# The second plane of a unit in two VectorE instructions: one bank, then two banks

## The chip, the cores and the metric

One core of one Trainium2 chip runs the whole program. The time is the device time of that core in microseconds (us); the kernel before was run three times and the median counts. Tensors lie in SBUF (128 partitions) and in PSUM, 128 partitions with 8 banks of 512 fp32 each. Engines: TensorE (PE; its weight loads PEld), VectorE (DVE), ScalarE (ACT), GpSimd (POOL), SyncE (SP, which issues the DMAs). They run side by side and meet only at semaphores.

## The reference

A decoder of two layers on 32 batches of 56 tokens with a context of 1500 rows, width 128: self attention, cross attention, experts, a state-space block, the second cross attention and experts again. The change is in the second cross attention:

```python
xn = _layernorm(x, ln_gamma, ln_beta)
q = (xn @ w_q).reshape(B, SQ, NUM_HEADS, DIM_HEAD)      # 32, 56, 16 heads, 64
kv = context @ w_kv                                     # 32, 1500, ...
k, v = jnp.split(kv, 2, axis=-1)
...
scores = jnp.einsum('bqhd,bkhd->bhqk', q * SCALE, k)
attn = jax.nn.softmax(scores, axis=-1)
out = jnp.einsum('bhqk,bkhd->bqhd', attn, v).reshape(B, SQ, INNER)
out = out @ w_out + b_out
return out * jnp.tanh(gate[0])
```

## The kernel before

`cross_attention_phase` multiplies the queries by the key weights beforehand, so that scores come straight from the context, and applies value and output weights behind the attention. A *unit* is 128 rows of scores (8 tokens by 16 heads) by 1500 context columns. A batch has 7 units, a pair of batches 14 (NU), and there are 16 pairs, 224 units in all. The first and the last pair are written out, the 14 between are a loop; inside a pair the position s runs from 0 to 13.

Scores of unit s stand in three PSUM banks, 500 columns in each: banks 0 to 2 for even s, 3 to 5 for odd s (`bank = 3 * (s % 2)`). A unit goes through these steps:

- TensorE, `scores` (L2098 to L2100): for each bank three matmuls, high by high, high by low and low by high parts. Ahead of the group of bank j it waits on `h2_ready` until unit s-2, which used the same bank, is done with it.
- VectorE, `maximum`: a maximum over two banks (L2226) as soon as they are there, then one over the third bank and the first result (L2230).
- ScalarE, `exponentials` (L2344): the exponentials of all three banks in place, with their sum.
- VectorE, `inverse` (L2235, L2237): the sum's reciprocal.
- ScalarE, `high_part` (L2360): the normalised probabilities in fp16 into plane 0 of `h`, in two instructions: banks 0 and 1, then bank 2. Each adds to `h1_ready`.
- VectorE, `low_part` (L2245): probability times reciprocal minus plane 0 gives the rest, plane 1 of `h`, in three scalar_tensor_tensor instructions of one bank each. Each adds one to `h2_ready`, and with that frees its bank for unit s+2.
- SyncE transposes `h` by DMA into `prT` (L1971) once all of `h2_ready` is there; for two units of a pair TensorE transposes (`turn`, L2148, in three rounds of eight) and VectorE copies (`keep_turned`, L2251).
- TensorE, `values` (L2123 to L2125): probabilities by context, seven units behind.

The order on each engine is written by hand in its `step`. TensorE in position s: scores of s, a third or a quarter of the value matmuls of a group, then at some positions something more: projection of the next pair's queries (L2083, positions 2 to 5), output matmuls of the previous pair (L2158, positions 7 to 9), its transpose and logits (positions 12 and 13), a turn (positions 0, 1, 6, 10, 11, 13). VectorE in position s: `inverse` of s-1, copies of a turn (positions 0, 1, 2, 7, 11, 12), at position 10 the residual, `maximum` of s, `low_part` of s-1, at position 11 the normalisation.

Of the kernel before, what the change touches and what calls it, by code (L numbers as in the profile page):

```python
# [21 lines left out]
ALU = mybir.AluOpType  # L22
# [19 lines left out]
def this(i, n=1, per=1):  # L42

    return i * per + (per + n)
# [136 lines left out]
def open_sems(engine, per, *sems):  # L181

    for s in sems:
        engine.sem_inc(s, per)
# [1651 lines left out]
def cross_attention_phase(k):  # L1836

    nc = k.nc
    W = C // 3
    UQ = 128 // H1  # L1840
    UPS = S // UQ
    NU = 2 * UPS
# [9 lines left out]
    H_SLOT = [0, 1, 2, 0, 3, 1, 2, 0, 1, 2, 0, 3, 1, 2]  # L1852
# [6 lines left out]
    SCALE = DH1 ** -0.5  # L1859
    P_ONE, N_ONE, TINY = 16384.0, 8192.0, 1.0e-25  # L1860
    PIECES = [(j * W, (j + 1) * W) for j in range(3)]
    with ExitStack() as ctx:
        t = Tail(k, ctx, "xa", router=k.router1, per=1)
        sem = lambda name: k.sem(ctx, "xa_" + name)
# [6 lines left out]
        h = sb("h", [128, 4, 2, CP], fp16)  # L1871
        prT = sb("prT", [128, 2 * GA + UPS - GA, 2 * KT, 128], fp16)
        ident16 = sb("ident16", [128, 128], fp16)
        negmax, rs, rinv = sb("negmax", [128, 2, 1]), sb("rs", [128, 2, 1]), sb("rinv", [128, 2, 1])
# [4 lines left out]
        psum = ctx.enter_context(nc.psum_tensor("xa_psum", [128, 8, 512], fp32))  # L1879
# [8 lines left out]
        h1_ready, h2_ready = sem("h1_ready"), sem("h2_ready")  # L1888
# [53 lines left out]
        @block.sync  # L1942
        def _(sp):
            def load_T(i, h_):

                sp.wait_ge(c_lo_ready, this(i, h_, 2))
                sp.sem_inc(issuing, 1)
                sp.dma_start(ctxT[:, :].unsqueeze(1),
                             k.dram["ctxT"][bass.ds(2 * i + h_, 1), :, :].rearrange("b d c -> d b c"))\
                    .then_inc(ctxT_loaded, 16)  # L1950

            def load_P(i, h_):

                sp.wait_ge(n_lo_ready, this(i, h_, 2))
                sp.sem_inc(issuing, 1)
                sp.dma_start(ctxP[:, :].unsqueeze(1),
                             k.dram["ctxP"][bass.ds(2 * i + h_, 1), :, :, :].rearrange("b q t d -> q b (t d)"))\
                    .then_inc(ctxP_loaded, 16)

            def transpose(i, s):  # L1960

                sp.wait_ge(h2_ready, this(i, 3 * s + 3, 3 * NU))
                sp.sem_inc(issuing, 1)
                b, u = s // UPS, s % UPS

                if u < GA:
                    sp.wait_ge(pv_ready, last(i, 2 * b + 1, NG))
                else:
                    sp.wait_ge(pv_ready, this(i, 2 * b, NG))
                sp.sem_inc(issuing, 1)  # L1970
                sp.dma_start_transpose(prT[:, P_SLOT[s], :, :], h[:, H_SLOT[s], :, :].rearrange("p a c -> p (a c)"))\  # L1971
                    .then_inc(transposed[s], 16)

            def step(i, s, end=False):
                if s not in TURNED:
                    transpose(i, s)
                if s == 1 and not end:
                    load_T(i + 1, 0)
                if s == 4:
                    load_P(i, 1)  # L1980
                if s == 8 and not end:
                    load_T(i + 1, 1)
                if s == 11 and not end:
                    load_P(i + 1, 0)

            load_T(0, 0)
            load_P(0, 0)
            load_T(0, 1)
            with sp.Fori(0, PAIRS - 1) as i:
                for s in range(NU):  # L1990
                    step(i, s)
            for s in range(NU):
                step(PAIRS - 1, s, end=True)
# [78 lines left out]
        def _(pe):  # L2072
# [14 lines left out]
            def scores(i, s):  # L2087
                b, p0, bank = s // UPS, (s % UPS) * UQ, 3 * (s % 2)
                if s % UPS == 0:
                    pe.wait_ge(q_lo_ready, this(i, b + 1, 2))  # L2090
                    pe.wait_ge(c_lo_ready, this(i, b + 1, 2))
                qh = q_hi[:, b, p0:p0 + UQ, :].rearrange("p a b -> p (a b)")
                ql = q_lo[:, b, p0:p0 + UQ, :].rearrange("p a b -> p (a b)")
                for j, (a, z) in enumerate(PIECES):

                    pe.wait_ge(h2_ready, this(i, 3 * (s - 2) + j + 1, 3 * NU))
                    out = psum[:, bank + j, 0:W]
                    nc.tensor.matmul(out, qh, c_hi[:, b, a:z], start=True, stop=False)  # L2098
                    nc.tensor.matmul(out, qh, c_lo[:, b, a:z], start=False, stop=False)  # L2099
                    done = nc.tensor.matmul(out, ql, c_hi[:, b, a:z], start=False, stop=True)  # L2100
                    if j:
                        done.then_inc(scores_ready, 1)
# [26 lines left out]
            def turn(i, u, r, first=False, end=False):  # L2129

                if r:
                    pe.wait_ge(turn_kept[u], this(i, r, NR))
                else:
                    pe.wait_ge(h2_ready, this(i, 3 * u + 3, 3 * NU))
                if u == TURNED[0] and r == 0:
                    pe.wait_ge(turn_kept[TURNED[1]], last(i, NR, NR))
                    if not end:
                        pe.wait_ge(q_kept, q_count(i + 1, NB - 1))
                if u == TURNED[0] and r == 1 and not first:
                    pe.wait_ge(t.r_ready, this(i - 1))  # L2140
                if u == TURNED[1] and r == 0:
                    pe.wait_ge(turn_kept[TURNED[0]], this(i, NR, NR))
                    if not first:
                        pe.wait_ge(t.logits_kept, this(i - 1))
                for j in range(KT // NR):
                    for x in range(2):
                        kt = r * (KT // NR) + j
                        done = nc.tensor.transpose(turn_bank[:, j, x, :], h[:, H_SLOT[u], x, kt * 128:(kt + 1) * 128],  # L2148
                                                   ident16[:, :])
                done.then_inc(turn_ready[u], 1)  # L2150
# [64 lines left out]
        @block.vector  # L2215
        def _(dve):
            open_sems(dve, NU, two_ready, max_ready, total_ready, rinv_ready)
            open_sems(dve, 3 * NU, h2_ready)
            open_sems(dve, NR, *turn_kept.values())
            t.open_vector(dve)  # L2220

# [17 lines left out]
            def low_part(i, s):  # L2239
                bank = 3 * (s % 2)  # L2240
                dve.wait_ge(rinv_ready, this(i, s + 1, NU))
                for j, (a, z) in enumerate(PIECES):
                    if j != 1:
                        dve.wait_ge(h1_ready, this(i, 2 * s + (1 if j == 0 else 2), 2 * NU))
                    nc.vector.scalar_tensor_tensor(h[:, H_SLOT[s], 1, a:z], psum[:, bank + j, 0:W], rinv[:, s % 2, :],  # L2245
                                                   h[:, H_SLOT[s], 0, a:z], ALU.mult, ALU.subtract).then_inc(h2_ready, 1)

            def keep_turned(i, u, r):

# [336 lines left out]
```

## Time and profile before

| | us |
|---|---|
| median of three runs | 1936.44 |
| lowest, highest | 1933.33, 1942.58 |
| the profiled execution | 1935.19 |
| its span, first to last instruction | 1933.5 |
| TensorE busy (share of the span) | 1715.1 (89%) |
| VectorE busy | 1557.1 (81%) |
| ScalarE busy | 1184.6 (61%) |
| GpSimd busy | 797.9 (41%) |
| the 672 instructions of L2245 | 452.6 |
| the 224 of L2226 and the 224 of L2230 | 269.6 and 154.9 |

Busy time is a sum over the program; which engine an end waits for has to be read stage by stage. The chain of work that ended last covers only the very end of the program here (its shares read 0%), so it says nothing on this stage. A matmul's duration on the page overlaps the next one's; the distance between starts is what a matmul costs in a row of many. The second cross attention takes more than half of the span.

### The profile page before, as it was taken

To read this page: it belongs to the slowest core of one execution; us is meant where nothing else is said; L and a number is where in the kernel's file an instruction comes from. 1 tells how busy PE (TensorE), PEld (TensorE's weight loads), DVE (VectorE), ACT (ScalarE), POOL (GpSimd) and SP (SyncE) were. 2 spreads that over 40 slices of the span, in tenths; PEclk is the share of its full clock that TensorE was granted. 3 is DMA by queue.
4 is the path that set the end of the run, shared out by engine and by line. 5 is a ranking of instruction groups with operands and counts; after the bars stand their busy time and mean duration, and the time that the engine had idled before them with its cause. 6 is when DMAs were issued, how large, how long until landed. Compare 5 with 4: busy or idle time off the path is not lost. (4 is left out here: it accounts for less than half of the span.)

```text
span 1933.5 us, 33921 instructions
## 1 busy us (share of the span) xinstructions
PE 1715.1 (89%) x10135; PEld 1224.0 (63%) x10135; DVE 1557.1 (81%) x2940; ACT 1184.6 (61%) x1869; POOL 797.9 (41%) x674
## 2 busy tenths in 40 slices
PE   4887996899946599999999999999999999994997
PEld 2554665777722457666666766666676676663886
DVE  4985785677756498998899899889989988985886
ACT  2432332787721477777777777777777777764553
POOL 4640111233332554554636445463544536321333
PEclk9987998799976699999999999999999999997998
DMA  5202884221100398888898888989888898983231
GB/s 184 93 0 100 328 335 183 57 54 45 23 1 0 100 208 188 187 178 196 175 192 180 186 187 178 200 172 193 178 186 188 178 197 175 183 154 116 47 78 29
DMA packets 632491, 281.86 MB, mean 146 GB/s; under 512 B 602076, under 2 KB 606460, under 8 KB 631676
## 3 DMA queue, kind: packets, MB, share of 16 engines
q1 hardware_dynamic: 632428, 281.10, 62.4%
q8 instruction: 30, 0.49, 0.1%
q14 instruction: 33, 0.27, 0.0%
HBM read 129.02 MB, written 1.05 MB: 67 GB/s over the span
## 5 line engine op out<-in xcount | busy, mean ns | idle before, releaser
L2344 ACT ACTIVATE xa_psum<-xa_psum,xa_negmax 128x1500 f32<-128x1500 f32 x224 | 332.7, 1485 | 197.0 <-DVE xa_negmax L2230 197.0
L2245 DVE SCALAR_TENSOR_TENSOR xa_h<-xa_psum,xa_rinv,xa_h 128x500 f16<-128x500 f32 x672 | 452.6, 729 | 0.7 <-ACT xa_h L2360 0.7
L2360 ACT ACTIVATE xa_h<-xa_psum,xa_rinv 128x1000 f16<-128x1000 f32 x448 | 372.1, 882 | 82.5 <-DVE xa_rinv L2237 81.2
L2226 DVE TENSOR_REDUCE xa_psum<-xa_psum 128x1 f32<-128x1000 f32 x224 | 269.6, 1204 | 86.8 <-PE xa_psum L2100 86.7
L2098 PE MATMUL xa_psum<-xa_c_hi,xa_q_hi 128*128 128x500 f32 x672 | 282.1, 420 | 29.2 <-DVE xa_h L2245 19.0
L2123 PE MATMUL xa_psum<-xa_prT,xa_n_hi 128*128 128x512 f16 (+1 forms) x768 | 272.9, 355 | 1.8 <-issue 1.0
L2125 PE MATMUL xa_psum<-xa_prT,xa_n_lo 128*128 128x512 f16 (+1 forms) x768 | 270.7, 352 | 0.0
L2124 PE MATMUL xa_psum<-xa_prT,xa_n_hi 128*128 128x512 f16 (+1 forms) x768 | 270.7, 352 | 0.0
L2100 PE MATMUL xa_psum<-xa_c_hi,xa_q_lo 128*128 128x500 f32 x672 | 261.7, 389 | 0.0
L2099 PE MATMUL xa_psum<-xa_c_lo,xa_q_hi 128*128 128x500 f32 x672 | 261.5, 389 | 0.0
L2230 DVE TENSOR_REDUCE xa_negmax<-xa_psum 128x1 f32<-128x512 f32 x224 | 154.9, 692 | 25.8
L2017 POOL CAST xa_q_hi<-xa_q_full 128x896 fp32r<-128x896 f32 x32 | 29.8, 931 | 346.6 <-PE xa_psum L2100 335.6
L2098 PEld LDWEIGHTS xa_psum<-xa_c_hi,xa_q_hi 128*128 128x128 f32 x672 | 127.0, 189 | 72.2 <-DVE xa_h L2245 32.4
L1432 DVE TENSOR_TENSOR moe_hid_lo<-moe_hid,moe_hid_hi 128x448 fp32r<-128x448 f32 x200 | 125.2, 650 | 39.5 <-ACT moe_hid_hi L1551 34.1
L2100 PEld LDWEIGHTS xa_psum<-xa_c_hi,xa_q_lo 128*128 128x128 f32 x672 | 126.6, 188 | 26.0
L2123 PEld LDWEIGHTS xa_psum<-xa_prT,xa_n_hi 128*128 128x128 f16 x768 | 76.0, 99 | 103.7 <-issue 54.3
L2037 POOL TENSOR_SCALAR xa_ctxP<-xa_ctxP,xa_n_scale 128x1536 f32<-128x1536 f32 x32 | 133.3, 4167 | 17.8 <-DMA xa_ctxP<-in_ctxP 17.8
L2099 PEld LDWEIGHTS xa_psum<-xa_c_lo,xa_q_hi 128*128 128x128 f32 x672 | 127.4, 190 | 11.4
L2125 PEld LDWEIGHTS xa_psum<-xa_prT,xa_n_lo 128*128 128x128 f16 x768 | 75.1, 98 | 70.0
L1288 POOL TENSOR_TENSOR moe_acc<-moe_acc,moe_part 128x448 f32<-128x448 f32 x52 | 63.5, 1220 | 117.0 <-DVE moe_part L1475 62.6
L2030 POOL TENSOR_TENSOR xa_c_lo<-xa_ctxT,xa_c_hi 128x1500 fp32r<-128x1500 f32 x32 | 107.9, 3373 | 2.6
L2124 PEld LDWEIGHTS xa_psum<-xa_prT,xa_n_hi 128*128 128x128 f16 x768 | 75.5, 98 | 49.1
(304 smaller groups left out, 3465.3 us busy)
## 6 DMA issues: line engine op xcount, KB each, us to landing
ctxN<-in_ctxP SPq DMA_DIRECT2D x16, 1536.0 KB, 9.2
xa_ctxP<-in_ctxP SPq DMA_DIRECT2D x32, 768.0 KB, 4.3
ctxT<-in_ctxT SPq DMA_DIRECT2D x16, 1500.0 KB, 6.2
xa_ctxT<-in_ctxT SPq DMA_DIRECT2D x32, 750.0 KB, 4.7
moe_spread<-weight_rows SPq DMA_DIRECT2D x16, 1024.0 KB, 8.6
xa_prT<-xa_h SPq DMA_TRANSPOSE x192, 5.5
up<-in_F_up SPq DMA_DIRECT2D x1, 2048.0 KB, 9.2
down<-in_F_down SPq DMA_DIRECT2D x1, 2048.0 KB, 13.3
```

The costliest lines, as they stand in the source:

```text
L2037: pool.tensor_scalar(ctxP[:, :], ctxP[:, :], n_scale[:, :], None, ALU.mult).then_inc(n_scaled, 1)
L2098: nc.tensor.matmul(out, qh, c_hi[:, b, a:z], start=True, stop=False)
L2099: nc.tensor.matmul(out, qh, c_lo[:, b, a:z], start=False, stop=False)
L2100: done = nc.tensor.matmul(out, ql, c_hi[:, b, a:z], start=False, stop=True)
L2123: nc.tensor.matmul(out, nh, ph, start=(kt == 0), stop=False)
L2124: nc.tensor.matmul(out, nh, pl, start=False, stop=False)
L2125: done = nc.tensor.matmul(out, nl, ph, start=False, stop=(kt == KT - 1))
L2226: nc.vector.tensor_reduce(psum[:, bank + 1, W:W + 1], psum[:, bank:bank + 2, 0:W], AX.XY, ALU.max)\
L2230: nc.vector.tensor_reduce(negmax[:, s % 2, :], flat_psum[:, top:top + 512], AX.X, ALU.max, negate=True)\
L2245: nc.vector.scalar_tensor_tensor(h[:, H_SLOT[s], 1, a:z], psum[:, bank + j, 0:W], rinv[:, s % 2, :], h[:, H_SLOT[s], 0, a:z], ALU.mult, AL ...
L2344: nc.scalar.activation(psum[:, bank:bank + 3, 0:W], psum[:, bank:bank + 3, 0:W], ACT.Exp, bias=negmax[:, s % 2, :], accum_out=rs[:, s % 2, ...
L2360: nc.scalar.activation(h[:, H_SLOT[s], 0, a * W:z * W].rearrange("p (a c) -> p a c", c=W), psum[:, bank + a:bank + z, 0:W], ACT.Identity, ...
```

## The change

`low_part` makes plane 1 in two instructions: bank 0 alone, then banks 1 and 2 in one, with 1000 columns. Each waits for the ScalarE instruction with that count (`h1_ready`), so the wide one waits for plane 0 of bank 2 before it begins. `h2_ready` now rises by two per unit and no longer by three; TensorE's groups of the second and the third bank wait for the same count. All others that wait for a whole unit (the DMA transpose, the turn) count two. Nothing else is moved, and the arithmetic is the same.

```diff
+    LOW_PIECES = ((0, 1), (1, 3))
+    NL = len(LOW_PIECES)
...
-                sp.wait_ge(h2_ready, this(i, 3 * s + 3, 3 * NU))
+                sp.wait_ge(h2_ready, this(i, NL * (s + 1), NL * NU))
...
-                    pe.wait_ge(h2_ready, this(i, 3 * (s - 2) + j + 1, 3 * NU))
+                    pe.wait_ge(h2_ready, this(i, NL * (s - 2) + min(j + 1, NL), NL * NU))
...
-                    pe.wait_ge(h2_ready, this(i, 3 * u + 3, 3 * NU))
+                    pe.wait_ge(h2_ready, this(i, NL * (u + 1), NL * NU))
...
-            open_sems(dve, 3 * NU, h2_ready)
+            open_sems(dve, NL * NU, h2_ready)
...
-                for j, (a, z) in enumerate(PIECES):
-                    if j != 1:
-                        dve.wait_ge(h1_ready, this(i, 2 * s + (1 if j == 0 else 2), 2 * NU))
-                    nc.vector.scalar_tensor_tensor(h[:, H_SLOT[s], 1, a:z], psum[:, bank + j, 0:W], rinv[:, s % 2, :],
-                                                   h[:, H_SLOT[s], 0, a:z], ALU.mult, ALU.subtract).then_inc(h2_ready, 1)
+                for j, (a, z) in enumerate(LOW_PIECES):
+                    dve.wait_ge(h1_ready, this(i, 2 * s + j + 1, 2 * NU))
+                    high, low = (h[:, H_SLOT[s], x, a * W:z * W].rearrange("p (a c) -> p a c", c=W) for x in range(2))
+                    nc.vector.scalar_tensor_tensor(low, psum[:, bank + a:bank + z, 0:W], rinv[:, s % 2, :], high,
+                                                   ALU.mult, ALU.subtract).then_inc(h2_ready, 1)
```

VectorE in the loop, one position, before (`xa_h` is `h`, `xa_psum` the PSUM banks, `xa_rinv` the reciprocal):

```order
L2226 TENSOR_REDUCE xa_psum<-xa_psum 128x1
L2228 REGISTER_ALU
L2229 REGISTER_ALU
L2230 TENSOR_REDUCE xa_negmax<-xa_psum 128x1
L2245 SCALAR_TENSOR_TENSOR xa_h<-xa_psum,xa_rinv,xa_h 128x500 x3
L2235 TENSOR_SCALAR xa_total<-xa_rs 128x1
L2237 RECIPROCAL xa_rinv<-xa_total 128x1
```

The same place in the changed program:

```order
L2228 TENSOR_REDUCE xa_psum<-xa_psum 128x1
L2230 REGISTER_ALU
L2231 REGISTER_ALU
L2232 TENSOR_REDUCE xa_negmax<-xa_psum 128x1
L2247 SCALAR_TENSOR_TENSOR xa_h<-xa_psum,xa_rinv,xa_h 128x500
L2247 SCALAR_TENSOR_TENSOR xa_h<-xa_psum,xa_rinv,xa_h 128x1000
```

Three rows of 500 columns have become one of 500 and one of 1000; what stands around them is the same.

TensorE in the loop, the scores of one unit, before (`REGISTER_ALU` of L2096 works out the count that the next group waits for):

```order
L2096 REGISTER_ALU
L2098 MATMUL xa_psum<-xa_c_hi,xa_q_hi 128x500
L2099 MATMUL xa_psum<-xa_c_lo,xa_q_hi 128x500
L2100 MATMUL xa_psum<-xa_c_hi,xa_q_lo 128x500
L2096 REGISTER_ALU
L2098 MATMUL xa_psum<-xa_c_hi,xa_q_hi 128x500
L2099 MATMUL xa_psum<-xa_c_lo,xa_q_hi 128x500
L2100 MATMUL xa_psum<-xa_c_hi,xa_q_lo 128x500
L2096 REGISTER_ALU
L2098 MATMUL xa_psum<-xa_c_hi,xa_q_hi 128x500
L2099 MATMUL xa_psum<-xa_c_lo,xa_q_hi 128x500
L2100 MATMUL xa_psum<-xa_c_hi,xa_q_lo 128x500
```

And in the changed program:

```order
L2098 REGISTER_ALU
L2100 MATMUL xa_psum<-xa_c_hi,xa_q_hi 128x500
L2101 MATMUL xa_psum<-xa_c_lo,xa_q_hi 128x500
L2102 MATMUL xa_psum<-xa_c_hi,xa_q_lo 128x500
L2098 REGISTER_ALU
L2100 MATMUL xa_psum<-xa_c_hi,xa_q_hi 128x500
L2101 MATMUL xa_psum<-xa_c_lo,xa_q_hi 128x500
L2102 MATMUL xa_psum<-xa_c_hi,xa_q_lo 128x500
L2100 MATMUL xa_psum<-xa_c_hi,xa_q_hi 128x500
L2101 MATMUL xa_psum<-xa_c_lo,xa_q_hi 128x500
L2102 MATMUL xa_psum<-xa_c_hi,xa_q_lo 128x500
```

No matmul has moved; the third group has no count of its own any more, since it waits for the same one as the second.

## Rows read from the trace of the kernel before

**Rows 1.** Windows: bounds, length, busy us (instructions), PEclk, DMA share, GB/s.

```profile
656.00:1733.00 1077.00, 1056.01 (x6015) 728.59 (x6015) 974.46 (x1736) 807.33 (x1108) 539.29 (x279) 1.00 0.88 183
1121.50:1189.30 67.80, 67.10 (x388) 46.41 (x386) 61.12 (x110) 50.66 (x71) 34.39 (x19) 1.00 0.88 185
660.00:670.00 10.00, 6.36 (x34) 5.22 (x34) 9.49 (x17) 8.37 (x13) 9.75 (x4) 1.00 0.60 94
670.00:680.00 10.00, 7.42 (x39) 6.07 (x40) 9.54 (x17) 9.26 (x15) 0.62 (x1) 1.00 1.02 236
```

**Rows 2.** Timeline (start, duration, instruction): pair's first scores, position 5, next pair.

```profile
1121.53 0.48 PE L2098 MATMUL xa_psum<-xa_c_hi,xa_q_hi 128*128 128x500 f32 x1
1144.27 2.02 DVE L2245 SCALAR_TENSOR_TENSOR xa_h<-xa_psum,xa_rinv,xa_h 128x500 f16<-128x500 f32 x3
1145.59 0.48 PE L2098 MATMUL xa_psum<-xa_c_hi,xa_q_hi 128*128 128x500 f32 x1
1147.24 1.21 DVE L2226 TENSOR_REDUCE xa_psum<-xa_psum 128x1 f32<-128x1000 f32 x1 [0.68 <-PE xa_psum L2100]
1149.18 2.02 DVE L2245 SCALAR_TENSOR_TENSOR xa_h<-xa_psum,xa_rinv,xa_h 128x500 f16<-128x500 f32 x3
1150.49 0.48 PE L2098 MATMUL xa_psum<-xa_c_hi,xa_q_hi 128*128 128x500 f32 x1
1189.39 0.49 PE L2098 MATMUL xa_psum<-xa_c_hi,xa_q_hi 128*128 128x500 f32 x1
```

**Rows 3.** Waits of the whole program: waiting <- awaited, us in total, times, longest.

```profile
DVE xa_psum L2226 <- PE xa_psum L2100: 86.7, 115, 22.9
PEld xa_psum L2098 <- DVE xa_h L2245: 32.4, 56, 3.2
PE xa_psum L2098 <- DVE xa_h L2245: 19.0, 24, 2.8
```

**Rows 4.** Timeline of position 13 of the pair before that one.

```profile
1113.71 1.66 ACT L2360 ACTIVATE xa_h<-xa_psum,xa_rinv 128x1000 f16<-128x1000 f32 x2 [0.91 <-DVE xa_rinv L2237]
1116.09 2.02 DVE L2245 SCALAR_TENSOR_TENSOR xa_h<-xa_psum,xa_rinv,xa_h 128x500 f16<-128x500 f32 x3
1116.88 0.50 PE L2098 MATMUL xa_psum<-xa_c_hi,xa_q_hi 128*128 128x500 f32 x1 [0.61 <-DVE xa_h L2245]
1117.62 0.19 ACT L2344 ACTIVATION_READ_ACCUMULATOR xa_psum<-xa_psum,xa_negmax 128x1 f32 x1
1117.67 0.39 PE L2098 MATMUL xa_psum<-xa_c_hi,xa_q_hi 128*128 128x500 f32 x1
1118.03 0.14 DVE L2235 TENSOR_SCALAR xa_total<-xa_rs 128x1 f32<-128x1 f32 x1
1118.35 0.38 PE L2098 MATMUL xa_psum<-xa_c_hi,xa_q_hi 128*128 128x500 f32 x1
1118.55 1.21 DVE L2226 TENSOR_REDUCE xa_psum<-xa_psum 128x1 f32<-128x1000 f32 x1 [0.18 <-PE xa_psum L2100]
```

**Rows 5.** Groups by line and form: count, busy us, mean ns, idle before.

```profile
L2245 DVE SCALAR_TENSOR_TENSOR xa_h<-xa_psum,xa_rinv,xa_h 128x500 f16<-128x500 f32 x672 | 452.6, 729 | 0.7 <-ACT xa_h L2360 0.7
L1475 DVE SCALAR_TENSOR_TENSOR moe_part<-moe_psum,down_bias,moe_spread 128x448 f32<-128x448 f32 x28 | 19.1, 681 | 6.4 <-PE moe_psum L1348 5.7 <-issue 0.3
L2259 DVE SCALAR_TENSOR_TENSOR xa_r<-xa_psum,gate_tanh,xa_xg 128x128 f32<-128x128 f32 x16 | 5.6, 351 | 14.6 <-PE xa_psum L2158 14.5
L2226 DVE TENSOR_REDUCE xa_psum<-xa_psum 128x1 f32<-128x1000 f32 x224 | 269.6, 1204 | 86.8 <-PE xa_psum L2100 86.7
L2230 DVE TENSOR_REDUCE xa_negmax<-xa_psum 128x1 f32<-128x512 f32 x224 | 154.9, 692 | 25.8
```

**Rows 6.** Timeline of the first unit, where VectorE was free.

```profile
658.63 0.19 ACT L2344 ACTIVATION_READ_ACCUMULATOR xa_psum<-xa_psum,xa_negmax 128x1 f32 x1
658.86 0.15 DVE L2235 TENSOR_SCALAR xa_total<-xa_rs 128x1 f32<-128x1 f32 x1 [1.67 <-ACT xa_psum L2344]
```

**Rows 7.** Timeline of the first pair, positions 3 and 4.

```profile
665.24 2.02 DVE L2245 SCALAR_TENSOR_TENSOR xa_h<-xa_psum,xa_rinv,xa_h 128x500 f16<-128x500 f32 x3
666.03 0.50 PE L2098 MATMUL xa_psum<-xa_c_hi,xa_q_hi 128*128 128x500 f32 x1 [1.11 <-DVE xa_h L2245]
667.70 1.21 DVE L2226 TENSOR_REDUCE xa_psum<-xa_psum 128x1 f32<-128x1000 f32 x1 [0.18 <-PE xa_psum L2100]
670.33 0.49 PE L2098 MATMUL xa_psum<-xa_c_hi,xa_q_hi 128*128 128x500 f32 x1 [1.12 <-DVE xa_h L2245]
```

## The prediction

> **What bounds the kernel now.** I read the busy time by stretch first, then the waits, then the timeline of single units. The second cross attention runs from about 652 to 1740 us. In it TensorE was busy 1056 of 1077 us, VectorE 974, ScalarE 807, and TensorE's granted clock was 1.00, its 2.4 GHz level [rows 1]. One pair of batches (14 units, positions 0 to 13) takes 67.86 us, from the start at 1121.53 to the one at 1189.39 [rows 2]; TensorE is busy 67.10 of 67.80 us there, VectorE 61.12 [rows 1]. So TensorE sets the pace in most positions, and VectorE only now and then: TensorE waits for the second plane of a unit (L2245) 80 times, 51.4 us in all, and VectorE waits for scores 115 times, 86.7 us [rows 3].
>
> The timeline shows both kinds of position. Call L the start of the first L2245 of unit s-2, which frees the banks that unit s needs, and "lead" the start of the scores of unit s minus L. At position 13 VectorE is last: L is 1116.09, the scores start at 1116.88 and have waited [rows 4]. So a finished bank (0.73 us long) is seen 0.06 us after its end, at L+0.79. At position 5 TensorE is last: L is 1144.27, the scores start at 1145.59 (lead 1.32), and the next ones 4.90 us later, with no gap [rows 2]. Read in the same way, the leads of the pair are 0.96, 0.78, 0.79, 0.95, 1.31, 1.31, 1.31, 0.92, 1.48, 1.52, 1.52, 0.83, 0.79, 0.78 for positions 0 to 13 (14 pairs of rows, of which [rows 2] has position 5 and [rows 4] position 13 of the pair before). Only those at 0.78 and 0.79 wait for the first bank.
>
> **Part 1, one instruction less.** Three L2245 lie 0.646 us apart: (2.02-0.73)/2, with a single one of 729 ns [rows 4, 5]. An instruction of two banks is not in the trace. Scalar_tensor_tensor takes 351 ns for 128 columns and 681 for 448 [rows 5], 1.03 ns per column; 729 plus 500 columns gives 1.245. The maximum over the same two banks and 1000 columns takes 1204 against 692 for 512 [rows 5], 1.05 per column, so reading over two banks costs nothing extra; that gives 1.254. I take 1.25. Bounds: 1.19 by the slope between 448 and 500 columns (48 ns for 52), and 1.375, two narrow ones (0.646+0.729), if nothing is saved. The wide one then holds VectorE for 1.25-0.729+0.646 = 1.167 us in place of 1.292. Saved: 0.125 us per unit, 224 units, 28.0 us of VectorE.
>
> Does the next instruction profit? It waits for ScalarE's sum. When VectorE was free, it began 0.04 us after that sum's end (658.63+0.19 to 658.86) [rows 6]; at position 13 the sum ends at 1117.81 and it began at 1118.03 [rows 4], so it can come 0.18 us earlier, and the whole 0.125 is usable. The second wait of the new form (ScalarE's third bank, before the wide one rather than before the third) is covered: the second ScalarE instruction had ended at 1113.71+1.66 = 1115.37, before L = 1116.09 [rows 4]. What this is worth alone: the waits of TensorE at the four positions with lead 0.78 to 0.79 come to 1.15 us per pair, start to start (67.80-67.10 is 0.70, to which the tails of four overlapping matmuls are added). Walking the pair with banks freed as before and VectorE 0.125 faster gives 67.2 for 67.7, so 8 us over the phase.
>
> The Trainium skill, page "VectorE: DVE Perf Modes", section "The TRN2 errata — SBUF-src ops pay a fixed extra latency per instruction", says that the fixed cost lies between instructions and that a large tile pays it once. The three rows 0.646 us apart agree as to the fixed part. Followed alone it would have the change gain what VectorE saves.
>
> **Part 2, the release of banks.** Scores of unit s go bank by bank, three matmuls each. TensorE needs the second bank 0.79 us after its start when it waited, 0.77 when it didn't, and the third 0.68 later [rows 4]. Before, the second bank was free at L+0.646+0.729+0.06 = L+1.43, always in time. Now it comes with the third, at L+0.646+1.25+0.06 = L+1.95. A scores start with lead x therefore stalls for 1.95-(x+0.77) where that is positive: 0.40 us at 0.78, 0.35 at 0.83, 0.26 at 0.92, nothing from 1.18 on. To it comes a restart of 0.10: the first matmul after a wait takes 0.50 and its group 0.79, where a group in the flow takes 0.68 [rows 4] (bound below: 0). Queued behind the stalled matmul are the rest of the scores, the value matmuls, projections and turns of that position, and VectorE's maximum, which needs the second bank's scores: it starts 0.88 after the second bank's first matmul (1117.67 to 1118.55) [rows 4]. The maximum then holds up ScalarE's exponentials and everything of the next unit.
>
> **The sum.** I walked the 14 positions: TensorE's own time in each (4.90 with a projection, the others from start to start in the same manner), the scores not before L+0.78, the maximum 0.88 behind, the next L another 1.93 to 1.94 behind the maximum (1147.24 to 1149.18) [rows 2], VectorE's other steps as they are. For the kernel before, this gives 67.70 us per pair against 67.86 measured: 66.55 of own work and 1.15 of waits. For the changed one the leads settle at 1.08, 1.02, 1.05, 1.42, 1.32, 1.32, 1.32, 0.91, 1.83, 1.52, 1.52, 0.85, 1.01, 0.78. The stalls with restarts are 0.20, 0.25, 0.23 at positions 0 to 2, 0.37 at 7, 0.43 at 11, 0.26 at 12 and 0.50 at 13, together 2.24, and 0.08 of the old wait is left: 66.55+2.24+0.08 = 68.87. So a pair loses 1.17 us, and 14 inner pairs 16.4.
>
> In the first pair TensorE has no value matmuls for seven positions and waits in almost all: L 665.24, scores 666.03, maximum 667.70, next scores 670.33, a position every 4.30 us [rows 7]. Now the maximum can start at L+1.95+0.88 = L+2.83, not L+2.46, so each such position costs 0.37. There are ten of them in the first pair and five in the last (no projections): 5.6. Sum: 22.0 us on the profiled execution's span of 1933.5, so 1955.5; the whole execution had 1935.19 and the median of the three runs is 1936.44, 2.9 above the span: 1958.4.
>
> **The rivals.** (a) The wide instruction is shorter than I think. At 1.19 the walk gives +15, without the restart cost +12: 1949. For: the shallow slope up to 500 columns. Against: 1.05 ns per column over two banks [rows 5].
> (b) It ends on the other side: VectorE sets the pace and the late release costs nothing. That needs the second bank by L+1.55, a wide instruction of 0.85 us, or TensorE always more than 1.18 behind L. Then only part 1 is left: -8 us, 1928; with all of TensorE's 1.15 per pair and the gaps of the first pair it could reach -20, 1917. This is what the skill's rule taken alone would give. For it: 80 waits of TensorE for VectorE. Against: seven of 14 leads are under 1.0.
> (c) Gain and loss cancel: at a wide instruction of 1.03 us the walk breaks even, 1936. No row is near that.
> (d) Two banks in one instruction save nothing (1.375): the walk gives +38, 1974. Against: the maximum's rows.
> That the clock falls through the new stalls is not among them: from 660 to 680 us TensorE was busy 64 to 74% and had 1.00 [rows 1].
>
> **How the numbers follow.** A measurement here tells 0.5%, 9.7 us, from no change. Forecast 0.66 (slower), (a) 0.12 (slower, a third of it within 0.5%), (b) 0.10 (0.04 of it faster by over 0.5%, the rest within), (c) 0.07 (within), (d) 0.05 (slower). That makes faster 0.04, same 0.16, slower 0.80. The range goes from 1944, below (a), to 1967, which takes a wide instruction of 1.30.
>
> **What would show it.** The new row of 128x1000 at 1.25 us; VectorE's busy time down by 28; waits of TensorE at the second bank's first matmul, none of which exist now, seven per pair, about 0.1 to 0.5 us each; those at the first bank nearly gone; VectorE's wait for scores not smaller although it has less to do; pairs of 68.9 us. A pair under 67.9 or no waits at the second bank would prove the step on the release wrong.

## The result and the profile after

The changed kernel takes **1966.95 us** (median of four runs, 1965.76 to 1971.38). Four runs of the kernel before, on the same chip, have a median of 1938.31 (1933.33 to 1942.58). The ratio is 1.0153 with a 95% interval of 1.0122 to 1.0183: slower by 28.6 us, where 22.0 were forecast. The profiled execution took 1971.38 us, its span is 1969.5.

First the busy time by stretch, one pair of batches and then the whole stage; the columns are those of [rows 1].

```profile
1100.00:1169.40 69.40, 68.39 (x386) 45.87 (x385) 59.87 (x96) 50.47 (x70) 34.47 (x18) 1.00 0.86 181
656.00:1733.00 1077.00, 1050.27 (x5819) 699.61 (x5820) 924.01 (x1462) 778.51 (x1075) 534.81 (x275) 1.00 0.86 179
```

In one pair VectorE is busy for 59.87 us, where it was 61.12. The second row is the same stretch of time as before and not the same work: the changed kernel gets less far in it, so only part of the step from 974 to 924 us is work saved. TensorE still has its 2.4 GHz (1.00) over the stage as a whole. Then the forms of L2247 (L2245 before), the maximum and the waits, against [rows 5] and [rows 3]. Columns: busy us, mean ns | idle before it, and for the waits us in total, times, longest.

```profile
L2247 DVE SCALAR_TENSOR_TENSOR xa_h<-xa_psum,xa_rinv,xa_h 128x1000 f16<-128x1000 f32 x224 | 279.9, 1250 | 0.0
L2247 DVE SCALAR_TENSOR_TENSOR xa_h<-xa_psum,xa_rinv,xa_h 128x500 f16<-128x500 f32 x224 | 163.2, 729 | 0.7 <-ACT xa_h L2362 0.7
L2228 DVE TENSOR_REDUCE xa_psum<-xa_psum 128x1 f32<-128x1000 f32 x224 | 270.4, 1207 | 136.1 <-PE xa_psum L2102 130.5
```

```profile
ACT xa_psum L2346 <- DVE xa_negmax L2232: 251.7, 224, 11.8
DVE xa_psum L2228 <- PE xa_psum L2102: 130.5, 155, 22.9
PEld xa_psum L2100 <- DVE xa_h L2247: 84.0, 149, 2.8
PE xa_psum L2100 <- DVE xa_h L2247: 16.6, 47, 2.4
```

VectorE's instruction count and time fell, and the waits for the release and for the maximum grew. The two rows of TensorE for plane 1 come to 196 waits and 100.6 us, where they were 80 and 51.4. (Each of the two sums adds the waits of weight loads and of matmuls, which stand side by side: at 1137.91, in the next timeline, one stall counts 0.64 us for the load and 0.23 for the matmul. So they show the direction, not the time lost.) VectorE waits for scores 130.5 us, not 86.7.

The timeline of position 13 (start, duration, instruction; the counterpart of [rows 4]) shows where.

```profile
1135.96 1.90 DVE L2247 SCALAR_TENSOR_TENSOR xa_h<-xa_psum,xa_rinv,xa_h 128x500 f16<-128x500 f32 x2
1136.74 0.49 PE L2100 MATMUL xa_psum<-xa_c_hi,xa_q_hi 128*128 128x500 f32 x1 [0.15 <-DVE xa_h L2247]
1137.48 0.19 ACT L2346 ACTIVATION_READ_ACCUMULATOR xa_psum<-xa_psum,xa_negmax 128x1 f32 x1
1137.77 0.14 DVE L2237 TENSOR_SCALAR xa_total<-xa_rs 128x1 f32<-128x1 f32 x1
1137.91 0.50 PE L2100 MATMUL xa_psum<-xa_c_hi,xa_q_hi 128*128 128x500 f32 x1 [0.23 <-DVE xa_h L2247]
1138.70 0.38 PE L2100 MATMUL xa_psum<-xa_c_hi,xa_q_hi 128*128 128x500 f32 x1
1138.90 1.21 DVE L2228 TENSOR_REDUCE xa_psum<-xa_psum 128x1 f32<-128x1000 f32 x1 [0.78 <-PE xa_psum L2102]
```

L is 1135.96. The first bank's scores start at L+0.78, as before. The second bank's start at L+1.95, 1.17 behind the first bank's and no longer 0.79, and VectorE is idle for 0.78 us before the maximum may begin. Position 3 of the next pair is one whose scores come late enough to find all three banks free:

```profile
1155.55 1.90 DVE L2247 SCALAR_TENSOR_TENSOR xa_h<-xa_psum,xa_rinv,xa_h 128x500 f16<-128x500 f32 x2
1156.86 0.47 PE L2100 MATMUL xa_psum<-xa_c_hi,xa_q_hi 128*128 128x500 f32 x1
1157.62 0.39 PE L2100 MATMUL xa_psum<-xa_c_hi,xa_q_hi 128*128 128x500 f32 x1
1158.29 0.39 PE L2100 MATMUL xa_psum<-xa_c_hi,xa_q_hi 128*128 128x500 f32 x1
1158.49 1.21 DVE L2228 TENSOR_REDUCE xa_psum<-xa_psum 128x1 f32<-128x1000 f32 x1 [0.79 <-PE xa_psum L2102]
```

Put side by side, the two timelines hold what the prediction left out. In both the maximum starts 0.20 us after the third bank's first matmul (1138.70 to 1138.90, 1158.29 to 1158.49). From the second bank's first matmul to the third's it is 0.67 us in position 3 (1157.62 to 1158.29), but 0.79 in position 13 (1137.91 to 1138.70), where that first matmul has waited and takes 0.50. So the maximum comes 0.99 us behind the second bank's first matmul where that has waited, and 0.87 where it hasn't.

A pair now takes 69.44 us, from maximum to maximum (the median of the inner pairs); before it was 67.83. The whole stage is bounded by the first and the last maximum (columns: shortest, median and longest ns, then first and last start). Before:

```profile
L2226 DVE TENSOR_REDUCE xa_psum<-xa_psum x224: 1189/1208/1208, 655.2 to 1726.3; 128x1 f32<-128x1000 f32 x112
```

After:

```profile
L2228 DVE TENSOR_REDUCE xa_psum<-xa_psum x224: 1189/1208/1208, 660.1 to 1762.7; 128x1 f32<-128x1000 f32 x112
```

That is 1071.1 and 1102.6 us: 31.5 longer. Another 4.9 of the 36.0 us between the two spans lie ahead of the first maximum, in code that is the same in both. The last section comes back to them; the profiled execution was the longest of its four.

### The profile page after: what moved, and what is told of

Its sections match the earlier page's. It is cut to its first block and busy times, and to the rows that moved or that the text cites. A ratio compares the mean times of both kernels' runs of the same rounds, so it can differ in the third digit from the quotient of the medians.

```text
span 1969.5 us, 33501 instructions
## 1 busy us (share of the span) xinstructions
PE 1744.6 (89%) x10135; PEld 1218.7 (62%) x10135; DVE 1538.4 (78%) x2716; ACT 1181.2 (60%) x1869; POOL 798.1 (41%) x674
## 5 line engine op out<-in xcount | busy, mean ns | idle before, releaser
L2247 DVE SCALAR_TENSOR_TENSOR xa_h<-xa_psum,xa_rinv,xa_h 128x500 f16<-128x500 f32 x448 | 424.6, 989 | 0.7 <-ACT xa_h L2362 0.7
L2228 DVE TENSOR_REDUCE xa_psum<-xa_psum 128x1 f32<-128x1000 f32 x224 | 270.4, 1207 | 136.1 <-PE xa_psum L2102 130.5
L2100 PE MATMUL xa_psum<-xa_c_hi,xa_q_hi 128*128 128x500 f32 x672 | 294.7, 439 | 35.0 <-DVE xa_h L2247 16.6
## 6 DMA issues: line engine op xcount, KB each, us to landing
down<-in_F_down SPq DMA_DIRECT2D x1, 2048.0 KB, 13.4
```

Source lines behind the costliest of these rows:

```text
L2228: nc.vector.tensor_reduce(psum[:, bank + 1, W:W + 1], psum[:, bank:bank + 2, 0:W], AX.XY, ALU.max)\
L2247: nc.vector.scalar_tensor_tensor(low, psum[:, bank + a:bank + z, 0:W], rinv[:, s % 2, :], high, ALU.mult, ALU.subtract).then_inc(h2_ready, 1)
```

## The experiments

Two theories differ in one point. **Theory 1**, formed from the two timelines above: the late release sets the time, and a score group that has waited runs 0.11 us longer, so that the maximum of that unit is later by as much, and with it everything of the next unit. A unit whose second bank waits then can't take less than 1.95 to the release, 0.99 to the maximum and 1.93 to the next L: 4.87 us. **Theory 1a** is the prediction's: the same without that delay (0.88, so 4.76). **Theory 2**: not the release but the wide instruction as such makes the kernel slower, wherever it stands. For Theory 1 and 1a I walked the 14 positions as in the prediction. Since the 0.99 was read from the changed kernel's own trace, only the kernels below can test it. Each is compared with runs of the kernel before on its own chip.

**Late release without the wide instruction.** The kernel before, with its three narrow instructions; only the second bank's scores wait for the third one.

```diff
-                    pe.wait_ge(h2_ready, this(i, 3 * (s - 2) + j + 1, 3 * NU))
+                    pe.wait_ge(h2_ready, this(i, 3 * (s - 2) + (3 if j else 1), 3 * NU))
```

> The kernel before, with its three one-bank instructions untouched; only TensorE's group of the second bank waits for the third instruction, as its third group does. So VectorE saves nothing and the release is late: L+0.646+0.646+0.729+0.06 = L+2.08. Theory 1 (the late release costs, and the restart of 0.10 delays the second bank's scores too, so that a position with lead 0.78 takes 2.08+0.98+1.93 = 4.99 us from L to L): the walk gives 70.2 us per pair and +47 us. Theory 1a (the restart counts for TensorE alone, as in the prediction): 69.8 per pair, +39. Theory 2 (the instruction over two banks is itself the cost, whatever waits for it): no such instruction here, so 0.

Measured: 1988.09 us against 1937.04, ratio 1.0257 (1.0242 to 1.0273), so 51 us slower, and 70.7 us per pair. Its timeline in a position with a late start of scores:

```profile
1103.93 2.02 DVE L2245 SCALAR_TENSOR_TENSOR xa_h<-xa_psum,xa_rinv,xa_h 128x500 f16<-128x500 f32 x3
1105.24 0.47 PE L2098 MATMUL xa_psum<-xa_c_hi,xa_q_hi 128*128 128x500 f32 x1
1106.01 0.49 PE L2098 MATMUL xa_psum<-xa_c_hi,xa_q_hi 128*128 128x500 f32 x1
1106.99 1.21 DVE L2226 TENSOR_REDUCE xa_psum<-xa_psum 128x1 f32<-128x1000 f32 x1 [0.78 <-PE xa_psum L2100]
```

No wide instruction runs here, and a wait on the release alone costs more than the whole change did. Theory 2, which had 0, falls. The release is at L+2.08 (1103.93 to 1106.01), which is 0.77 after the scores' start, just when TensorE wants the bank. The matmul comes no later than in the flow, and still the maximum is 0.98 behind: its group pays the 0.11 of one that has waited. What waited was the weight load of this group (last section). That makes each of these units 2.08+0.98+1.94 = 5.00 us; measured are 4.99 to 5.02 in ten of the 14 positions. The walk of Theory 1 took such a tie for free at positions 3 to 6; four times 0.11 more makes its 70.2 us per pair 70.6, for 70.7 measured. That is worked out afterwards and explains most of the step from 47 to 51. Theory 1a's 39 is further off.

**The wide instruction first.** Banks 0 and 1 are made together, then bank 2; the total saved on VectorE is the same.

```diff
-    LOW_PIECES = ((0, 1), (1, 3))
+    LOW_PIECES = ((0, 2), (2, 3))
...
-                    pe.wait_ge(h2_ready, this(i, NL * (s - 2) + min(j + 1, NL), NL * NU))
+                    pe.wait_ge(h2_ready, this(i, NL * (s - 2) + max(j, 1), NL * NU))
```

> The changed kernel with the wide instruction first (banks 0 and 1, then bank 2), TensorE's first two groups waiting for the first. VectorE's saving and the number of wide instructions are as in the changed kernel. Theories 1 and 1a: TensorE waits once, ahead of the first bank, until L+1.25+0.06 = L+1.31, and then runs through; the cycle at a waiting position is 1.31+0.79+0.88+1.93 = 4.91 us, and the walk gives 69.5 per pair and +34 us (no restart inside the scores, so 1 and 1a agree). Waits at the second group: none. Theory 2: the same as the changed kernel, +29 to +31.

Measured: 1974.52 us, ratio 1.0196 (1.0180 to 1.0211), 37.5 slower; 69.75 us per pair.

```profile
1102.63 1.90 DVE L2247 SCALAR_TENSOR_TENSOR xa_h<-xa_psum,xa_rinv,xa_h 128x1000 f16<-128x1000 f32 x2
1103.94 0.50 PE L2100 MATMUL xa_psum<-xa_c_hi,xa_q_hi 128*128 128x500 f32 x1 [0.19 <-DVE xa_h L2247]
1104.73 0.39 PE L2100 MATMUL xa_psum<-xa_c_hi,xa_q_hi 128*128 128x500 f32 x1
1105.62 1.21 DVE L2228 TENSOR_REDUCE xa_psum<-xa_psum 128x1 f32<-128x1000 f32 x1 [0.20 <-PE xa_psum L2102]
```

The stall has moved to where it was to move: the scores start at L+1.31 (the wide instruction's 1.25 and 0.06), the second bank follows without a wait, and the maximum comes at L+2.99. No stall inside a unit's scores is left, yet it is slower than the change. So it is not a stall in the middle of the scores as such that costs, but how far behind L the maximum comes. Theory 2 had 29 to 31 here. The time is 3.5 us above Theory 1: the waiting positions take the 4.91 us expected, positions 12 and 13 take 5.03 and 4.99, and where the rest comes from is open. The two versions of Theory 1 are not told apart here, since both charge the restart to the first bank as the prediction did.

**The wide instruction at some positions only.** Units 2, 3, 4, 6, 7 and 8 have the wide form, the others three narrow ones. At most of these TensorE comes late enough in the next unit but one to find the banks free. The second kernel has it at the other eight.

```diff
-    LOW_PIECES = ((0, 1), (1, 3))
-    NL = len(LOW_PIECES)
+    WIDE = (2, 3, 4, 6, 7, 8)
+    LOW_PIECES = [((0, 1), (1, 3)) if s in WIDE else ((0, 1), (1, 2), (2, 3)) for s in range(NU)]
...
```

> The wide instruction only for units 2, 3, 4, 6, 7 and 8 of a pair, whose banks are wanted by positions 4, 5, 6, 8, 9 and 10, where TensorE starts its scores 1.3 us or more after L; the other eight units keep three instructions. 96 of 224 are wide. Theories 1 and 1a: inner pairs as before (67.7 by the walk, 67.8 in the trace of before), +4 us in all, from the first and the last pair, where TensorE has little else to do. Theory 2: 6/14 of the changed kernel's loss, +12 to +13.

> The complement: wide for units 0, 1, 5 and 9 to 13 (128 of 224), three instructions for the other six. Theory 1: inner pairs as in the changed kernel (69.3 by the walk, 69.44 in its trace), +26 us in all. Theory 1a: +20. Theory 2: 8/14 of the loss, +16 to +17.

Measured: 1939.19 us, ratio 1.0012 (1.0003 to 1.0021), 2.2 slower, 67.75 us per pair, for the six; 1964.19, ratio 1.0148 (1.0132 to 1.0163), 27.2 slower, 69.39 per pair, for the eight. Together 29.3, the change's 28.6. In the inner pairs the cost lies where the scores start less than 1.18 behind L, and not in proportion to the number of wide instructions, which would have been 12 and 16. What the six cost is in the first and the last pair, where almost every position waits: their first pair took 64.10 us and not 61.18. And 27.2 is near Theory 1's 26, not Theory 1a's 20. But in the inner pairs the six covered positions gain next to nothing either, 0.08 us per pair (67.83 to 67.75) for 0.75 us saved on VectorE, since TensorE sets the pace in them.

**The saving without the release.** Three narrow instructions, the third over 380 of its 500 columns, which makes it shorter by the same 0.125 us (604 ns, not 729). Plane 1 of the last 120 context columns is left out. A second kernel leaves out 240.

```diff
+                    n = W - (120 if j == 2 else 0)
...
+                    nc.vector.scalar_tensor_tensor(h[:, H_SLOT[s], 1, a:a + n], psum[:, bank + j, 0:n], rinv[:, s % 2, :],
```

> The kernel before, with three instructions and every release in its place, but the third one covers 380 of its 500 columns (plane 1 of the last 120 context columns is left out of the result and stays zero). That takes 0.125 us per unit off VectorE, as the wide instruction does, and holds nothing back. Theory 1: the walk gives 67.2 us per pair in place of 67.7 and -8 us (0.4%). Rival 3 (VectorE's time sets nothing, TensorE is last everywhere): 0. Rival 4 (VectorE sets the pace, as its 28 us saved would say): -17 or more.

> As saving_alone, with 260 of 500 columns in the third instruction: 0.25 us per unit less for VectorE (240 context columns without plane 1). Theory 1: the next instruction waits for ScalarE's sum after 0.18 of it, so hardly more than the single saving: 67.1 per pair, -10 us. Rival 3: 0. Rival 4: -35.

Measured: 1928.51 against 1936.43 us, ratio 0.9956 (0.9944 to 0.9969), 7.9 faster, and 67.26 us per pair, where the walk of the prediction had 67.2 and 8 us. With twice the saving: 1922.99, ratio 0.9924 (0.9911 to 0.9937), 13.4 faster, 66.95 per pair. So 28 us less of VectorE are worth 7.9, and the next 28 another 5.5, where I had expected 2. (The missing columns make these two kernels' results incomplete; they price the time alone.) Why the second is worth less than the first shows in its timeline:

```profile
1113.60 1.77 DVE L2246 SCALAR_TENSOR_TENSOR xa_h<-xa_psum,xa_rinv,xa_h 128x500 f16<-128x500 f32 x3
1115.12 0.19 ACT L2345 ACTIVATION_READ_ACCUMULATOR xa_psum<-xa_psum,xa_negmax 128x1 f32 x1
1115.35 0.15 DVE L2235 TENSOR_SCALAR xa_total<-xa_rs 128x1 f32<-128x1 f32 x1
```

ScalarE's sum ends at 1115.31 and VectorE's next step begins 0.04 later, the latency of [rows 6]: at this place, position 13, VectorE has caught up with ScalarE's sum, and a shorter instruction would bring nothing more.

**One instruction for all three banks.** The release of every bank is the last one's.

```diff
-    LOW_PIECES = ((0, 1), (1, 3))
+    LOW_PIECES = ((0, 3),)
...
-                    dve.wait_ge(h1_ready, this(i, 2 * s + j + 1, 2 * NU))
+                    dve.wait_ge(h1_ready, this(i, 2 * s + 2, 2 * NU))
```

> The changed kernel with all three banks in one instruction of 1500 columns (0.729+1000 x 1.042 = 1.77 us) and one release for all. VectorE saves 0.25 us per unit. Theory 1: all banks come at L+1.83, TensorE waits in every position ahead of the first bank, the cycle is 1.83+0.79+0.88+1.93 = 5.43 us: 75.9 per pair, +137 us. A theory by the number and width of the instructions (twice the extra width of the changed kernel, so twice its loss) gives +58; one by VectorE's time a gain.

Measured: 2073.98 us (two runs), ratio 1.0710 (1.0691 to 1.0729), 137.6 slower, 76.06 us per pair.

```profile
1103.66 1.77 DVE L2247 SCALAR_TENSOR_TENSOR xa_h<-xa_psum,xa_rinv,xa_h 128x1500 f16<-128x1500 f32 x1
1105.48 0.49 PE L2100 MATMUL xa_psum<-xa_c_hi,xa_q_hi 128*128 128x500 f32 x1 [1.06 <-DVE xa_h L2247]
1107.15 1.21 DVE L2228 TENSOR_REDUCE xa_psum<-xa_psum 128x1 f32<-128x1000 f32 x1 [1.39 <-PE xa_psum L2102]
```

VectorE has 32 us less to do than in the kernel before (1525.0 us busy on its page, for 1557.1), and this kernel is the slowest of all. The loop is plain to see: L to the release 1.82, to the maximum 1.67, to the next L 1.94, 5.43 in all (2.02 and 5.51 in the position shown, the last of a pair). Theory 1's 137 is met, though in part by luck: the first pair took 78.71 us, 2.7 more than an inner one, with TensorE's granted clock at 0.50 for 20 us of it, and no walk has that.

**Taking work off VectorE in another way.** If VectorE's time is worth something only while the release stays early, a move of work away from VectorE helps the kernel before and not the changed one. VectorE also copies the turned probabilities (L2251), six copies of 0.69 us per pair. First all six go to ScalarE, ahead of its exponentials:

```diff
+            def keep_turned(i, u, r):
+
+                act.wait_ge(turn_ready[u], this(i, r + 1, NR))
+                nc.scalar.activation(
...
+                    turn_bank, ACT.Copy).then_inc(turn_kept[u], 1)
```

> The kernel before, with the six copies per pair of the turned units moved from VectorE to ScalarE, ahead of the exponentials of the same position. It tries the same aim (less for VectorE, 0.60 us in six positions) without touching a release. Theory 1: the walk with the copies gone gives 66.6 per pair, that is TensorE's own work, and at best -17 us. But ScalarE has to fit a copy of about 1.1 us into a gap of 0.8 us between plane 0 and the exponentials, so these start some 0.3 later in six positions; 0.18 of that is covered by the slack of its sum, which leaves -10 to -15. Rival: ScalarE becomes last in these positions, 0 or slower.

Measured: 1928.70 against 1936.43, ratio 0.9965 (0.9952 to 0.9978), 7.7 faster, below what I expected.

```profile
1129.37 1.02 ACT L2331 ACTIVATE xa_prT<-xa_psum 128x1024 f16<-128x1024 f16 x1
1130.45 0.34 PEld L2148 LDWEIGHTS xa_psum<-xa_ident,xa_h 128*128 128x128 f16 x6 [0.34 <-ACT xa_prT L2331]
```

The copy takes 1.02 us on ScalarE and stands behind `high_part` of the unit before; TensorE waits for it, for the bank of the turns is also that of projections and outputs. From maximum to maximum position 2 took 5.23 us and position 7 5.53, where the kernel before has 4.53 and 5.06. So these two copies stay on VectorE, and those of positions 0, 1, 11 and 12 move. The same is then done to the changed kernel:

> The kernel before with four of the six copies of a pair on ScalarE; the first one of the first turned unit (position 7) and the last one of the second (position 2) stay on VectorE, since TensorE waits for just these two to go on with outputs and projections in the same bank. With all six on ScalarE position 2 took 5.23 us and position 7 5.53, in place of 4.9 and 5.3 of TensorE's own work. Theory 1: the walk gives 66.6 us per pair and -16 us at best; with the late exponentials of four positions -10 to -16, so faster than copies_on_scalar (-8). Rival: the start of the exponentials decides, and it stays at -8.

> The changed kernel with the same four copies on ScalarE, 0.60 us less for VectorE in four positions of a pair on top of its own 28 us. Theory 1: in the changed kernel a waiting position is set by L, the release at L+1.95, the scores and the maximum (4.87 us), where VectorE's own work has no part; so the copies gained are worth nothing: 69.3 by the walk as without them, +31 against the kernel before. Rival (VectorE's time still counts): it gains as copies_split does, which would give +13 to +19.

Measured for the kernel before with four copies moved: **1923.30 against 1938.44, ratio 0.9927 (0.9912 to 0.9943), 15.1 faster**, 66.83 us per pair. For the changed kernel with the same move: 1966.06, ratio 1.0139 (1.0119 to 1.0159), 27.6 slower, 69.33 per pair. It gains 1 us, which the intervals (1.0122 to 1.0183 and 1.0119 to 1.0159) don't tell from nothing, by what is worth 15 to the other. Its position 0, from which a copy was moved away:

```profile
1136.59 1.90 DVE L2247 SCALAR_TENSOR_TENSOR xa_h<-xa_psum,xa_rinv,xa_h 128x500 f16<-128x500 f32 x2
1137.56 0.49 PE L2101 MATMUL xa_psum<-xa_c_hi,xa_q_hi 128*128 128x500 f32 x1
1138.54 0.49 PE L2101 MATMUL xa_psum<-xa_c_hi,xa_q_hi 128*128 128x500 f32 x1
1139.52 1.21 DVE L2228 TENSOR_REDUCE xa_psum<-xa_psum 128x1 f32<-128x1000 f32 x1 [0.77 <-PE xa_psum L2103]
```

Again 1.95 and 0.98. A unit of 4.87 to 4.88 us is a floor that moving VectorE's copies away doesn't lower: the time of the copy has become idle time, 0.77 us ahead of this maximum where the changed kernel has 0.15 at position 0. In the kernel before, position 0 went from 4.75 to 4.49 us (maximum to maximum) by the move, position 10 from 4.76 to 4.41 and position 11 from 5.01 to 4.62; with the late release none of them is under 4.87.

## Where the prediction held, and the step that failed

**In short.** The mechanism was as forecast; the step that failed is one term of the sum, the time from the second bank's first matmul to the maximum. It stands at 0.88 us, and where that matmul has waited it measures 0.99. With that value the same sum gives a loss of 29.3 us and not 22.0; measured are 28.6.

**The bound.** Right: TensorE's pace in most positions, VectorE's in a few. The two kernels with a shortened third instruction confirm it from the side that the change itself can't show: 28 us of VectorE are worth 7.9 us, against 8 by the walk.

**Part 1.** Right to the digit. The wide instruction takes 1250 ns for a forecast of 1.25 us; the busy time of the group of L2245 was 452.6 us and its successor's is 424.6 (448 instructions, on the page of the kernel after), down by 28.0. VectorE's total fell by 18.7 only (1557.1 to 1538.4), not by the 28 that were forecast for it. Most of the other 9.3 is a matter of counting: an instruction that follows another without a gap overlaps it by 0.08 us in the trace, and the total counts the overlap once. In the kernel before, 93 maxima follow a copy in this way, 7.8 us of overlap; in the changed kernel they wait for scores instead, and stand apart from it. The second wait is covered: the idle time before the wide form is 0.0 in the group above. The sum of ScalarE ends at 1137.67 and the next step begins at 1137.77, which is 0.10 later and not 0.22, so the 0.125 was usable. Rivals (a) and (d), a shorter or a longer wide instruction, are out by the same row, and so is (c).

**Part 2.** Right in its mechanism and its places: a release at L+1.95, and stalls at the second bank at just the seven positions named, 0 to 2, 7 and 11 to 13. Measured leads are 0.97, 0.91, 0.91, 1.31, 1.30, 1.32, 1.31, 0.93, 1.74, 1.52, 1.52, 0.90, 0.91 and 0.78, within 0.14 of the forecast ones. The second bank follows the first one's start after 0.98 to 1.17 us at the seven, after 0.77 at the others. Of the waits for the first bank one per pair is left (position 13, lead 0.78), and VectorE's wait for scores has grown, as was said.

**The term that was mis-sized** is the restart. The prediction says that "the first matmul after a wait takes 0.50 and its group 0.79, where a group in the flow takes 0.68", charges this 0.10 to TensorE seven times per pair, and then has the maximum start "0.88 after the second bank's first matmul". That 0.88 was read where the second bank had not waited. The same restart lies between a waiting second bank and the maximum, so it is 0.99. A waiting position is thus not 2.83+1.93 = 4.76 us but 2.94+1.93 = 4.87; measured are 4.87 to 4.89 at positions 0 to 2. With 0.99 the same walk gives 69.28 us per pair for 69.44 measured, where it gave 68.87, and in all 14 times 1.58 and 15 times 0.48, 29.3 us, for a measured 28.6 (31.5 within the stage of the profiled executions). The 0.99 comes from this trace; that eight wide instructions cost 27.2 us, where the walk with it had said 26 and the one without it 20, is the check from outside. Of the forecast's ten positions of the first pair at 0.37 each the same holds; positions 3 and 4 there, the counterpart of [rows 7]:

```profile
671.40 1.90 DVE L2247 SCALAR_TENSOR_TENSOR xa_h<-xa_psum,xa_rinv,xa_h 128x500 f16<-128x500 f32 x2
673.35 0.49 PE L2100 MATMUL xa_psum<-xa_c_hi,xa_q_hi 128*128 128x500 f32 x1 [0.22 <-DVE xa_h L2247]
674.33 1.21 DVE L2228 TENSOR_REDUCE xa_psum<-xa_psum 128x1 f32<-128x1000 f32 x1 [0.77 <-PE xa_psum L2102]
676.18 1.90 DVE L2247 SCALAR_TENSOR_TENSOR xa_h<-xa_psum,xa_rinv,xa_h 128x500 f16<-128x500 f32 x2
```

L to the maximum is 2.93 us, not 2.83, and the position 4.78, against 4.30 before: 0.48 more, which is the forecast 0.37 and the restart's 0.11. The end of the range had room for a wide instruction of 1.30 us but none for this term, and so the measured median stands at its edge (1966.95 for 1967) instead of well inside. The runs leave 0.16 us per pair of 69.44 unexplained. Two smaller readings were off as well: the 51.4 us of waits ahead of the sum add weight loads and matmuls of the same stalls, which the sum itself doesn't use, and the clock, which was held at 1.00 throughout, fell once, for 3.4 us of the first pair, though behind a wait for the first bank, which is no new stall (last section).

**Rival (b)**, the gain of 8 to 20 us, needed banks by L+1.55. Its first half is real: without the late release the saving is worth 7.9. The Trainium skill, page "VectorE: DVE Perf Modes", section "The TRN2 errata — SBUF-src ops pay a fixed extra latency per instruction", holds for the instruction itself, as the prediction quoted it: one fixed part less, and 0.125 us per unit less. What that does to the time of a kernel doesn't follow from it: here the experiments put its worth at 7.9 us, and the price of the later release at 36.5, an estimate that adds this to the 28.6.

**What became of the bound.** In the changed kernel a waiting position is a loop over two engines: release, scores, maximum, next L. VectorE's own work isn't its limit any more, nor is TensorE's: VectorE idles ahead of the maximum, for 0.14 to 0.16 us at positions 0, 1, 2, 7 and 11, where it also has a copy to make, and for 0.78 at position 13. (At position 12 it has no gap; there its own work is still last.) That is why four moved copies, worth 15.1 us before, bring 1 us there.

## What to carry to other kernels

Merging two instructions also merges their releases. Before doing it, find who waits for the first one and by how much it is covered: here 0.52 us of later release at seven of 14 positions cost more than four times what a shorter instruction gave (the estimate of 36.5 us for 7.9). When a wait is added to a row of matmuls, charge the restart on every path that goes through that row, to the consumer of the result too, and charge it even where the release comes just in time for the matmul: here a release 0.12 us ahead was early enough, one at the matmul's own time was not.

## What the runs showed of the hardware

**A restart is a cost of its own, and the weight load tells who pays it.** A group of three score matmuls takes 0.67 or 0.68 us in the flow and 0.78 or 0.79 when the release comes no earlier than its first matmul; in the kernel with the late release it was so at a tie (0.77 from the first bank's start, as in the flow, and 0.78 for the next group). The load of the second bank's first weights, in the changed kernel at position 13 and at position 3:

```profile
1137.91 0.19 PEld L2100 LDWEIGHTS xa_psum<-xa_c_hi,xa_q_hi 128*128 128x128 f32 x1 [0.64 <-DVE xa_h L2247]
1157.50 0.19 PEld L2100 LDWEIGHTS xa_psum<-xa_c_hi,xa_q_hi 128*128 128x128 f32 x1
```

And at the tie of the kernel with the late release:

```profile
1106.00 0.19 PEld L2098 LDWEIGHTS xa_psum<-xa_c_hi,xa_q_hi 128*128 128x128 f32 x1 [0.26 <-DVE xa_h L2245]
```

Both positions of the changed kernel have the release at L+1.95, and in both the load begins right then. At position 13 its matmul begins with it (1137.91) and the group takes 0.79. At position 3 the matmul comes 0.12 later (1157.62) and the group takes 0.67, as it does where the load is 0.23 ahead, in the flow. At the tie the load is 0.01 ahead (1106.00 to 1106.01) and the group takes 0.78. It is the same over twelve inner pairs of the changed kernel: the 84 groups whose load begins with the matmul take 0.77 to 0.80 us, the 84 with a load 0.12 or more ahead take 0.67 to 0.69. So a release hides its restart when it is 0.12 us ahead of the matmul; what lies between 0.02 and 0.12 these traces don't show. That the load itself is the cause is the plain reading of these rows, but no experiment isolates it.

**Columns over several banks.** Scalar_tensor_tensor takes 729, 1250 and 1771 ns for 500, 1000 and 1500 columns: 521 ns for 500 more, each time, with nothing for the bank's end. Over 120 columns less in one bank it is 125 ns (729 to 604), the same 1.04 ns per column.

**The clock at the start of the stage** differs between executions. From 665 to 670 us, in windows of the kernel before and of the one after:

```profile
665.00:670.00 5.00, 3.19 (x17) 2.62 (x17) 4.75 (x9) 4.20 (x7) 4.75 (x3) 1.00 1.10 168
```

```profile
665.00:670.00 5.00, 3.36 (x8) 2.69 (x9) 3.40 (x7) 4.08 (x6) 5.00 (x2) 0.66 0.15 29
```

From 620 to 655 us both have 0.50, the 1.2 GHz level, with TensorE idle in some stretches of 5 us and busy for up to 80% of others. The clock then rises to 1.00 at 657.4 us in the kernel before, 2.2 us after its first maximum, and at 663.2 in the kernel after, 3.1 us after its own. In the kernel before it stays there to the end of the stage. In the kernel after it falls once more:

```profile
663.20:666.60 3.40, 1.05 (x5) 0.54 (x3) 2.77 (x6) 2.81 (x5) 3.40 (x2) 1.00 0.00 0
666.60:670.00 3.40, 3.36 (x8) 2.69 (x9) 1.83 (x4) 2.64 (x4) 3.40 (x1) 0.50 0.21 43
```

Before the fall TensorE had stood 2.40 us waiting for the first plane 1 of the stage, until 666.64. The kernel before waits there too (its longest such wait is 2.8 us [rows 3]) and kept 1.00. At the lower level the first matmuls of its score groups take 0.62 us (668.06 and 669.31), where the kernel before has 0.50 at 666.03 [rows 7]. The fall is one candidate for the 0.9 us by which the first pair, at 66.87 us, is longer than the 61.18 of before and ten times 0.48. It is not peculiar to the late release: seven of the twelve profiled executions have such falls in the first pair, among them those of the kernel with the saving twice over and of the one with all copies on ScalarE, and none has one in a later pair. With one instruction for all banks it fell five times.

Over the twelve kernels of this study the first maximum comes between 653.6 and 660.1 us, with the code ahead of it unchanged. The 4.9 us ahead of the stage are such a difference between executions. Why executions reach the stage at such different times is open.
